# A graph layer and eight experts on one core: route and experts in one program, partial quads by their tiles

## The chip, the cores and the metric

One of the cores of a Trainium2 chip runs the whole kernel. The time is the device time of one execution in microseconds (us), taken from the core. TensorE is called PE, VectorE DVE, ScalarE ACT, GpSimd POOL and SyncE, which issues most DMAs, SP.

## The reference

The input is 12500 nodes of 256 features, with 200000 edges. A graph layer comes first, then a layer of eight experts of which each node uses one:

```python
x = x + gnn(layernorm(x), src, dst)          # gather by src, sum by dst, two products, batch norm
# then, with h = layernorm(x), C = ceil(1.25 * 12500 / 8) = 1954, D = 256, F = 1024:
probs = softmax(h @ gate_w + gate_b);  idx = argmax(probs);  prb = probs[idx]
pos = running count of idx;  kept = pos < C
buf = zeros((8, C, D)).at[idx, pos].set(h, mode='drop')
hmid = relu(einsum('ecd,edf->ecf', buf, w1) + b1[:, None, :])
ybuf = einsum('ecf,efd->ecd', hmid, w2) + b2[:, None, :]
x = x + nan_to_num(ybuf[idx, pos] * (prb * kept)[:, None])
```

By these inputs the experts get 1091, 1033, 3008, 980, 2266, 2418, 1025 and 679 nodes; at most 1954 of each are kept. In tiles of 128 nodes that is 9, 9, 16, 8, 16, 16, 9 and 6, or 89 in all.

## The kernel before

The program has four stages one after another: norm and edges (the graph layer, up to 1745 us in the profile), route (up to 1955 us) and experts (the rest).

**Route** (`stage_route`, L1142 on) goes over the nodes in quads of 4 tiles. It works out gate and position, stores the node itself to `out`, and scatters each node's row (features, statistics, node number, logits) to its slot in the DRAM buffer `slot_rows` (POOL, L1263), 512 slots to a quad and 4 quads to an expert. At its end SP issues the load of expert 0's weights (`load_expert`, L1136 to L1139) and waits for it. The stage is a block of its own: at the block's end (L1211) each engine drains its queue and all engines meet.

**Experts** (`stage_experts`) is a second block. SP loads the first slot's word of each tile (`first_row`, L1641), and DVE makes of them the number of used tiles of each expert, kept in `words`. Then 32 steps, one per quad, run on five engines with semaphores between them. The helper `walk` writes the order out: 8 steps, a loop of one round of 8 steps run twice (L130), and the last 8 steps with what drains. In a step each engine does its parts in the written order, each part for the quad that lies its lag behind:

```python
sp:   [(load, 0), (weights, 3)]                         # x_row in; next expert's weights
dve:  [(norm, 0), (meta, 0), (first_weights, 0), (split, 4), (finish, 3), (low_columns, 0)]
pe:   [(turn, 0), (product_up, 1), (product_down, 2)]
act:  [(expo, 0), (columns, 0), (hidden, 1), (split, 3)]
pool: [(low_hidden, 1), (scatter, 3)]
```

A quad goes through: `norm` (DVE L1827, `x_xn`, 4 instructions), `turn` (PE L1695, 8 transposes to PSUM `x_turned`), `columns` (ACT L1757, `x_xTh`, the f16 half), `low_columns` (DVE L1849, `x_xTl`, the rest), `product_up` (PE L1711, 8 chunks of 6 matmuls, as wide as the arm's tiles), `hidden` (ACT L1778, two activations a chunk), `low_hidden` (POOL L1659, `x_midl`), `product_down` (PE L1735, 24 matmuls a tile), `finish` (DVE L1878 to L1893: `yb` with the bias, `y` with the gate's share, then the guard for infinities and the sum into `x_res`) and `scatter` (POOL L1674, 4 indirect DMAs to `out`). The turn of quad s waits for `x_xn` of s and `x_xTl` of s-1; the down product of s waits for `yb` of s-1, since PSUM `x_down` holds one quad. `first_weights` and `split` divide an expert's weights in two f16 halves (ACT L1801, L1802; DVE L1841, L1843).

**Arms.** The number of used tiles is known to the engines only at run time. `branch` (L1597 to L1607) reads it and runs a quad or skips it. On PE alone there are two arms with code of their own, 4 tiles or 2. With the tile counts above PE works 4, 4, 2, 0 tiles in the quads of experts 0, 1 and 6, 4, 4, 0, 0 in expert 3, 4, 2, 0, 0 in expert 7, and 4 in each quad of the others: 92 tiles. The other engines work 25 full quads and skip 7; POOL scatters for all 32.

## Time and profile before

| | |
|---|---|
| median of 3 runs (lowest, highest) | 2583.26 us (2576.55, 2584.69) |
| the profiled execution, its span | 2588.4 us, 2586.6 us |
| mean granted clock of PE | 0.838 |
| PE, DVE, ACT, POOL busy | 1715.5, 1463.4, 693.4, 1737.4 us |

The profiled execution is one run more; its span is what its profile shows, and 1.8 us lie around it. A granted clock of 1 is TensorE's full 2.4 GHz, 0.5 is 1.2 GHz. Two thirds of the span are the graph layer, which the change leaves alone but for where buffers lie; what matters here is from 1740 us on. Below, a start time is in us from the start of the span, a name as `x_up<-x_xTh,x_w1h` says what is written out of what, a square bracket at the end is the engine's idle time before the row and what ended it, and engines with a q (PEq, POOLq) are their sequencers: there stand branches, drains and waits, which don't count as busy.

### The profile page before, as it was taken

The page shows a single profiled execution, that of the slowest core. Times are in us where ns is not written, and L with a number is a line of the kernel's source. Part 1 is how long each engine was busy: PE and PEld are TensorE (multiplying, and loading weights), DVE is VectorE, ACT ScalarE, POOL GpSimd, SP SyncE. Part 2 cuts the span into 40 slices and gives each one's busy share as a digit, 9 for nine tenths or more (in the row PEclk, how much of TensorE's full clock was granted, in tenths as well). Part 3 has the DMA queues.
Part 4 walks back from the last instruction along what each step waited for, and adds up shares of the span by engine and source line. Part 5 has one row for each costly group of instructions (what it writes and reads, how often), then busy time and mean ns, then how long its engine had stood idle before and what let it go on. Part 6 is the DMA issues. An engine that isn't in the chain of part 4 may idle for free. (4 is left out here: it accounts for less than half of the span.)

```text
span 2586.6 us, 32984 instructions
## 1 busy us (share of the span) xinstructions
PE 1715.5 (66%) x9167; PEld 1048.3 (41%) x9168; DVE 1463.4 (57%) x4301; ACT 693.4 (27%) x1092; POOL 1737.4 (67%) x1716
## 2 busy tenths in 40 slices
PE   0055446565667666677677777666656789899984
PEld 0033223233333333333333434345544556656663
DVE  7886632655247425633643333237873786857894
ACT  6910000100010001001110111116654545355552
POOL 1177777777777777777777776723563767677876
PEclk9986678777778888888789989986667989999997
DMA  7644466545744665466356433326753211222120
GB/s 231 237 135 119 122 202 204 158 131 171 234 153 123 192 221 151 131 199 213 96 171 211 128 105 93 105 50 209 222 164 106 88 49 56 94 84 72 49 93 13
DMA packets 202983, 361.16 MB, mean 140 GB/s; under 512 B 63573, under 2 KB 127403, under 8 KB 202790
## 3 DMA queue, kind: packets, MB, share of 16 engines
q0 software_dynamic: 70464, 185.02, 24.0%
q1 hardware_dynamic: 130182, 172.61, 20.6%
q8 instruction: 110, 1.80, 0.3%
q10 hardware_dynamic: 2144, 1.05, 0.2%
q14 instruction: 83, 0.68, 0.1%
HBM read 291.08 MB, written 75.58 MB: 142 GB/s over the span
## 5 line engine op out<-in xcount | busy, mean ns | idle before, releaser
L743 POOL DMA_INDIRECT e_got<-table,e_idx x1240 | 1188.4, 958 | 426.8 <-issue 366.2
L820 PE MATMUL e_sums<-e_got,e_hot 128*128 128x256 f16 x1920 | 358.2, 366 | 482.0 <-DMA e_got<-table,e_idx 276.7
L820 PEld LDWEIGHTS e_sums<-e_got,e_hot 128*128 128x128 f16 x1920 | 239.1, 128 | 606.0 <-DMA e_got<-table,e_idx 305.4
L1003 DVE SCALAR_TENSOR_TENSOR nodes<-e_sums,above,nodes 128x256 f32 (+1 forms) x161 | 77.3, 480 | 610.7 <-PE e_sums L820 396.1
L1659 POOL TENSOR_TENSOR x_midl<-x_midf,x_midh 128x512 f16<-128x512 f32 x200 | 294.3, 1498 | 97.6 <-ACT x_midh L1778 93.4
L926 ACT ACTIVATE e_hT<-e_up 128x1024 f32<-128x1024 f32 (+1 forms) x25 | 25.2, 1006 | 1074.8 <-PE e_up L869 1074.8
L1067 DVE TENSOR_TENSOR counts<-counts,e_tally 128x490 f32 x220 | 159.5, 725 | 127.7 <-PE e_tally L848 115.7
L1735 PE MATMUL x_down<-x_w2h,x_midh 128*128 128x256 f16 x736 | 205.4, 279 | 20.1 <-DVE x_yb L1878 8.1
L1735 PE MATMUL x_down<-x_w2h,x_midl 128*128 128x256 f16 x736 | 205.4, 279 | 0.0
L1735 PE MATMUL x_down<-x_w2l,x_midh 128*128 128x256 f16 x736 | 205.4, 279 | 0.0
L1674 POOL DMA_INDIRECT out<-x_res,x_nodei x128 | 144.9, 1132 | 88.4 <-DVE x_res L1893 49.7
L877 PE MATMUL e_up<-e_hT,W1s 128*128 128x512 f32 (+1 forms) x400 | 180.7, 606 | 28.6 <-ACT e_hT L926 28.6
L1017 DVE TENSOR_SCALAR e_hot<-ring,e_rel 128x128 f16 x960 | 175.5, 272 | 32.8 <-DVE e_rel L1011 32.5
L883 PE MATMUL e_up<-e_mid,W2s 128*128 128x512 f32 (+1 forms) x400 | 174.9, 590 | 19.2 <-ACT e_mid L929 19.2
L858 PE MATMUL e_tally<-w1f,counts 128*128 128x512 f16 x490 | 140.9, 428 | 49.4 <-DMA w1f<-table 48.3
L1263 POOL DMA_INDIRECT slot_rows<-r_row,r_slots x100 | 97.6, 976 | 92.6 <-DVE r_slots L1490 68.8
L1711 PE MATMUL x_up<-x_xTh,x_w1h 128*128 128x512 f16 (+1 forms) x400 | 149.3, 373 | 2.1 <-ACT x_midh L1778 2.1
L1711 PE MATMUL x_up<-x_xTh,x_w1l 128*128 128x512 f16 (+1 forms) x400 | 148.5, 371 | 2.3 <-issue 2.3
L1711 PE MATMUL x_up<-x_xTl,x_w1h 128*128 128x512 f16 (+1 forms) x400 | 148.8, 372 | 0.9 <-issue 0.9
L1778 ACT ACTIVATE x_midf<-x_up,x_b1s 128x512 f32<-128x512 f32 x200 | 138.7, 693 | 23.9 <-PE x_up L1711 15.5
L1778 ACT ACTIVATE x_midh<-x_up,x_b1s 128x512 f16<-128x512 f32 x200 | 137.6, 688 | 0.0
L848 PE MATMUL e_tally<-w2f 128*128 128x490 f16 x328 | 114.6, 458 | 28.4 <-DVE w2f L1056 27.3
(214 smaller groups left out, 2837.4 us busy)
## 6 DMA issues: line engine op xcount, KB each, us to landing
w1f<-table SPq DMA_DIRECT2D x120, 512.0 KB, 4.6
e_got<-table,e_idx POOLq DMA_INDIRECT x1240
slot_rows<-e_zero SPq DMA_DIRECT2D x64, 268.0 KB, 3.2
x_row<-slot_rows SPq DMA_DIRECT2D x32, 536.0 KB, 7.3
table<-n_pair SPq DMA_DIRECT2D x25, 512.0 KB, 2.9
counts<-in_x SPq DMA_DIRECT2D x24, 512.0 KB, 4.5
r_xin<-in_x SPq DMA_DIRECT2D x24, 512.0 KB, 5.0
out<-r_row SPq DMA_DIRECT2D x24, 512.0 KB, 3.2
```

The lines of the kernel that those rows point to most:

```text
L743: pool.indirect_dma_start(got[:, r, t, :], None, table.rearrange("p h d -> (p h) d"), bass.IndirectOffsetOnAxis(ap=idx[:, r, t:t + 1], axi ...
L820: ins = nc.tensor.matmul(sums[:, place, 0:D], hot[:, place, t, :], got[:, r, t, half * D:(half + 1) * D], start=(t == 0 and half == 0), st ...
L858: ins = nc.tensor.matmul(product, counts[:, k0 + k, 0:P], part[:, number % 2, k, :], start=(k0 + k == 0), stop=(k0 + k == HI - 1))
L877: ins = nc.tensor.matmul(up[:, c % 2, 0:width], W1s[:, j, c * P:(c + 1) * P], hT[:, j, 0:width], start=(j == 0), stop=(j == DK - 1))
L883: ins = nc.tensor.matmul(up[:, c, 0:width], W2s[:, j, c * P:(c + 1) * P], mid[:, j, 0:width], start=(j == 0), stop=(j == H1C - 1))
L1017: ins = nc.vector.tensor_scalar(hot[:, place, t, :], plan.ring[:, ring_at(shift)], rel[:, place, t:t + 1], None, ALU.is_equal)
L1067: nc.vector.tensor_tensor(place, place, tally[:, group % BANKS, 0:KEY].rearrange("p (k d) -> p k d", d=TW), ALU.add).then_inc(s_count, 1)
L1659: nc.gpsimd.tensor_tensor(midl[:, j % 2, c, :], midf[:, c % MB, :], midh[:, j % 2, c, :], ALU.subtract).then_inc(s_mlo, 1)
L1674: pool.indirect_dma_start(out, bass.IndirectOffsetOnAxis(ap=nodei[:, j, t:t + 1], axis=0), res[:, r, t, :], None, bounds_check=bound, oob_ ...
L1711: ins = nc.tensor.matmul(up[:, c % MB, 0:tiles * P], w[:, h, k, cols], x[:, j % 2, k, 0:tiles * P], start=(n == 0), stop=(n == len(passes) ...
L1735: ins = nc.tensor.matmul(down[:, t, :], m[:, j % 2, k, rows], w[:, h, k, :], start=(n == 0), stop=(n == len(passes) - 1))
L1778: ins = nc.scalar.activation(m, up[:, c % MB, :], ACT.Relu, bias=b1s[:, h, c:c + 1], scale=MID_SCALE / (X_SCALE * W_SCALE))
```

## The change

1. **One program.** Route's per-engine code becomes functions (`route.sync(sp)`, `route.tensor(pe)` and so on), which each engine runs ahead of its expert code in one block; the meeting of engines at L1211 is gone. Instead SP waits for the landing of `out` and of the scatters, and then issues `b2s` and the first `x_row`. The weights of expert 0 are issued at the start of route, and split there (ACT, DVE) into the memory `halves`, which the two stages and the graph layer share. The tile counts are worked out in route from its own counters.
2. **Norm and columns a step ahead.** All that follows `norm` lags a step more.
3. **The gate's share in the product out of PSUM.** `yb` and `y` become one step `product`, 4 instructions (a tile each) with the factor `share`; bias times share comes from ACT (`x_b2p`, 4 activations after `hidden`). The down product of s waits for it.
4. **Partial quads by their tiles.** `branch` takes a number of steps: 4 arms on PE, 2 for `hidden`, `low_hidden` and `finish`, 1 for `product` and `scatter`. A scatter of an unused quad sends 16 rows in place of 128.

```diff
-        with nc.Block() as block:
-            @block.sync
-            def _(sp):
-                sp.dma_start(gw[:, :, :], gate_w.rearrange("(k p) e -> p k e", p=P)).then_inc(s_gw, 16)
+        def route_sync(sp):
+            sp.dma_start(gw[:, :, :], gate_w.rearrange("(k p) e -> p k e", p=P)).then_inc(s_gw, 16)
+            load_expert(sp, nc, w1, xb1, w2, w1f, w2f, b1f, 0, s_w)
...
-                load_expert(sp, nc, w1, xb1, w2, w1f, w2f, b1f, 0, s_w)
-                sp.wait_ge(s_w, 48)
+            for j in range(R5):
+                sp.wait_ge(s_scat[j], 16 * QT * (NQ // R5))
...
-            def branch(own, j, work, skip, narrow=False):
+            def branch(own, j, work, skip, steps=1):
                 if j == 0:
                     engine.reg_mov(own, word)
                 used = engine.snap(engine.snap(own) % 32) if j < SG else engine.snap(engine.snap(own) // 32)
-                with engine.If(used > j % SG * QT):
-                    if narrow:
-                        with engine.If(used > j % SG * QT + QT // 2):
-                            work(QT)
-                        with engine.Else():
-                            work(QT // 2)
-                    else:
-                        work()
-                with engine.Else():
-                    skip()
+                base = j % SG * QT
+                def between(low, high):
+                    if high - low == 1:
+                        return work(high * QT // steps) if high else skip()
+                    middle = (low + high + 1) // 2
+                    with engine.If(used > base + (middle - 1) * QT // steps):
+                        between(middle, high)
+                    with engine.Else():
+                        between(low, middle)
+                between(-1, steps)
...
-                    branch(ups, j, work, skip, narrow=True)
+                    branch(ups, j, work, skip, QT)
...
-                            pe.wait_ge(s_yv, s * 7 - 6)
+                            pe.wait_ge(s_yv, (s - 1) * GUARD + 1)
...
-                walk(pe, [(take, 0), (turn, 0), (product_up, 1), (product_down, 2)], NS, R8)
+                walk(pe, [(take, 0), (turn, 1), (product_up, 2), (product_down, 3)], NS, R8)
...
+                        for t in range(QT):
+                            ins = nc.scalar.activation(b2p[:, j % 2, t, :], b2s[:, h, :], ACT.Identity,
+                                                       scale=prob[:, j, t:t + 1])
+                        ins.then_inc(s_b2p, 1)
...
-                walk(act, [(take, 0), (expo, 0), (columns, 0), (hidden, 1), (split, 3)], NS, R8)
+                walk(act, [(take, 0), (expo, 0), (columns, 1), (hidden, 2), (split, 4)], NS, R8)
...
+                def product(s, j, rnd):
+
+                    def work(tiles):
+                        dve.wait_ge(s_down, s + 1)
+                        dve.wait_ge(s_b2p, s + 1)
+                        if not (isinstance(s, int) and s == 0):
+                            dve.wait_ge(s_res, s)
+                        for t in range(tiles):
+                            ins = nc.vector.scalar_tensor_tensor(out=y[:, t, :], in0=down[:, t, :], scalar=share[:, j, t:t + 1],
+                                                                 in1=b2p[:, j % 2, t, :], op0=ALU.mult, op1=ALU.add)
+                        ins.then_inc(s_yv, 1)
...
-                walk(dve, [(take, 0), (norm, 0), (meta, 0), (first_weights, 0), (split, 4), (finish, 3), (low_columns, 0)], NS, R8)
+                walk(dve, [(take, 0), (product, 4), (low_columns, 1), (norm, 0), (meta, 0), (split, 5), (finish, 4)], NS, R8)
```

SP's order around the two boundaries. Before, expert 0's weights stand at the end of route, ahead of the block's end and the first loads of the experts:

```order
L1136 DMA w1f<-in_w 128x2x1024
L1137 DMA w2f<-in_w 128x8x256
L1139 DMA b1f<-in_xb 128x8x1
L1211 UNCONDITIONAL_BRANCH
L1613 UNCONDITIONAL_BRANCH
L1641 DMA x_first_row<-slot_rows 1x128x1
L1632 DMA x_b2s<-in_xb 128x256
L1637 DMA x_row<-slot_rows 128x4x268 x4
```

After the change SP begins route so:

```order
L1262 DMA r_gw<-in_gate_w 128x2x8
L1263 DMA r_gb<-in_gate_b 128x8
L1183 DMA w1f<-in_w 128x2x1024
L1184 DMA w2f<-in_w 128x8x256
L1186 DMA b1f<-in_xb 128x8x1
L1273 DMA r_xin<-in_x 128x4x256 x4
L1283 DMA out<-r_row 128x4x256
```

The weights have moved from behind route's last store to ahead of its first input, `r_xin`.

PE's up product of the first quad. Before, the arm of 4 tiles (512 wide) ends in a jump over the arm of 2 tiles:

```order
L1711 MATMUL x_up<-x_xTh,x_w1h 128x512
L1711 MATMUL x_up<-x_xTl,x_w1h 128x512
L1711 MATMUL x_up<-x_xTh,x_w1l 128x512
L1601 UNCONDITIONAL_BRANCH
L1711 MATMUL x_up<-x_xTh,x_w1h 128x256
L1711 MATMUL x_up<-x_xTl,x_w1h 128x256
L1711 MATMUL x_up<-x_xTh,x_w1l 128x256
```

After, PE's full arm of the same quad ends so (in `halves` lie the weights, and the rows with ISA are waits):

```order
L1790 MATMUL x_up<-x_xTl,halves 128x512
L1790 MATMUL x_up<-x_xTh,halves 128x512
L1667 UNCONDITIONAL_BRANCH
L1782 ISA
L1787 ISA
L1790 MATMUL x_up<-x_xTh,halves 128x384
```

Further on, still on PE, the arm of 3 tiles ends and that of 2 tiles begins, with a compare between them:

```order
L1790 MATMUL x_up<-x_xTl,halves 128x384
L1790 MATMUL x_up<-x_xTh,halves 128x384
L1669 UNCONDITIONAL_BRANCH
L1667 COMPARE_AND_BRANCH
L1782 ISA
L1787 ISA
L1790 MATMUL x_up<-x_xTh,halves 128x256
```

Last comes PE's arm of 1 tile, and behind it the skip (L1797) and the compares of the down product:

```order
L1790 MATMUL x_up<-x_xTl,halves 128x128
L1790 MATMUL x_up<-x_xTh,halves 128x128
L1667 UNCONDITIONAL_BRANCH
L1797 ISA
L1669 UNCONDITIONAL_BRANCH
L1660 ISA
L1667 COMPARE_AND_BRANCH x2
```

What has moved is where a jump leads: from the full arm PE now goes past three arms of 48 matmuls (144), before past one; in the down product past arms of 72, 48 and 24 matmuls (144 too), before past one of 48. A quad that is skipped goes past all four arms.

DVE's step in the first round. Before, the step of quad 3 and on reads so from its norm to the norm of the next:

```order
L1827 TENSOR_SCALAR x_xn<-x_row 128x256 x4
L1858 TENSOR_REDUCE x_tot<-x_ex 128x4
L1859 TENSOR_SCALAR x_gone<-x_row 128x4
L1862 RECIPROCAL x_prob<-x_tot 128x4
L1863 SCALAR_TENSOR_TENSOR x_nodei<-x_row,x_gone 128x4
L1597 ISA
L1599 COMPARE_AND_BRANCH
L1878 SCALAR_TENSOR_TENSOR x_yb<-x_down,x_b2s 128x1024
L1881 TENSOR_TENSOR x_y<-x_yb,x_prob 128x1024
```

After, DVE's step (at quad 4's norm) begins with the product of an earlier quad, and the guard of `finish` comes last:

```order
L1963 SCALAR_TENSOR_TENSOR x_y<-x_down,x_share,x_b2p 128x256 x4
L1667 UNCONDITIONAL_BRANCH
L1932 SCALAR_TENSOR_TENSOR x_xTl<-x_turned,x_xTh 128x1024
L1910 TENSOR_SCALAR x_xn<-x_row 128x256 x4
L1941 TENSOR_REDUCE x_tot<-x_ex 128x4
L1942 TENSOR_SCALAR x_gone<-x_row 128x4
L1945 RECIPROCAL x_prob<-x_tot 128x4
L1946 SCALAR_TENSOR_TENSOR x_nodei<-x_row,x_gone 128x4
L1949 TENSOR_SCALAR x_share<-x_prob 128x4
L1659 ISA
L1667 COMPARE_AND_BRANCH
L1986 TENSOR_SCALAR x_up<-x_y 128x1024
```

The read of PSUM `x_down` has moved to the step's head, ahead of `x_xTl` and `x_xn`; in the first quad of an expert it has no compare ahead of it, since its threshold is below any count.

## Rows read from the trace of the kernel before

**Rows 1.** Stretches: us, busy (and count) by engine, PE clock, DMA share, GB/s.
```profile
1745.00:1955.00 210.00, 115.41 (x1125) 100.23 (x1125) 156.34 (x680) 119.20 (x201) 100.40 (x105) 0.60 0.59 187
1955.00:2587.00 632.00, 538.18 (x3664) 373.66 (x3664) 450.19 (x512) 313.45 (x480) 440.67 (x329) 0.92 0.22 71
```

**Rows 2.** One line of ACT, 2410 to 2480 us: four full steps.
```profile
L1757 ACT ACTIVATE x_xTh<-x_turned x4: 1024/1024/1024, 2413.5 to 2478.7; 128x1024 f16<-128x1024 f32 x4
```

**Rows 3.** What PE waited for, 2000 to 2560 us: total, times, longest.
```profile
PE x_turned L1695 <- DVE x_xn L1827: 25.8, 6, 5.9
PE x_down L1735 <- DVE x_yb L1878: 8.1, 2, 4.1
PE x_down L1735 <- DVE x_dn L1885: 7.4, 2, 4.4
PE x_down L1735 <- PEq L1719: 4.6, 1, 4.6
```

**Rows 4.** The block's end, line L1211: count, ns min/median/max, start.
```profile
L1211 POOLq COMPARE_BRANCH  x1: 43/43/43, 1941.3 to 1941.3; - x1
L1211 POOLq DRAIN  x1: 8223/8223/8223, 1941.5 to 1941.5; - x1
```

**Rows 5.** Timeline from route's last scatter to the first quad.
```profile
1939.16 0.97 POOL L1263 DMA_INDIRECT slot_rows<-r_row,r_slots  x1 [0.30 <-issue]
...
1950.65 0.58 SPq L1632 DMA_DIRECT2D x_b2s<-in_xb  x1
...
1960.73 1.02 ACT L1757 ACTIVATE x_xTh<-x_turned 128x1024 f16<-128x1024 f32 x1 [2.63 <-PE x_turned L1695]
...
1961.29 2.28 DVE L1843 SCALAR_TENSOR_TENSOR x_w2l<-w2f,x_w2h 128x2048 f16<-128x2048 f32 x1
...
1963.50 1.22 DVE L1849 SCALAR_TENSOR_TENSOR x_xTl<-x_turned,x_xTh 128x1024 f16<-128x1024 f32 x1
```

**Rows 6.** Timeline of SP's DMAs at the start of route.
```profile
1741.46 2.21 SPq L1224 DMA_DIRECT2D r_xin<-in_x  x4
1753.25 0.38 SPq L1234 DMA_DIRECT2D out<-r_row  x1
```

**Rows 7.** What SP waited for, 1745 to 2587 us, one row.
```profile
SPq L1211 <- DMA b1f<-in_xb: 8.4, 1, 8.4
```

**Rows 8.** End of the work, timeline of POOL: first and last of 12 scatters.
```profile
2566.60 0.97 POOL L1674 DMA_INDIRECT out<-x_res,x_nodei  x1 [5.23 <-DVEq L1903]
...
2580.66 0.97 POOL L1674 DMA_INDIRECT out<-x_res,x_nodei  x1 [0.30 <-issue]
```

**Rows 9.** Groups by shape, 1955 to 2587 us: busy, mean ns, idle before.
```profile
L1735 PE MATMUL x_down<-x_w2h,x_midl 128*128 128x256 f16 x736 | 205.4, 279 | 0.0
...
L1881 DVE TENSOR_TENSOR x_y<-x_yb,x_prob 128x1024 f32<-128x1024 f32 x25 | 30.7, 1228 | 0.9
L1878 DVE SCALAR_TENSOR_TENSOR x_yb<-x_down,x_b2s 128x1024 f32<-128x1024 f32 x25 | 30.6, 1223 | 81.0 <-PE x_down L1735 80.6 <-issue 0.2
```

**Rows 10.** Timeline of PE, two up matmuls of a full arm.
```profile
1989.08 0.38 PE L1711 MATMUL x_up<-x_xTh,x_w1l 128*128 128x512 f16 x1
1989.30 0.38 PE L1711 MATMUL x_up<-x_xTh,x_w1h 128*128 128x512 f16 x1
```

**Rows 11.** PE's branches, by line and stretch: count, ns min/median/max, start.
```profile
L1601 PEldq COMPARE_BRANCH  x92: 65/171/3139, 1966.4 to 2547.6; - x92
...
L1601 PEldq COMPARE_BRANCH  x1: 3048/3048/3048, 2019.7 to 2019.7; - x1
...
L1599 PEldq COMPARE_BRANCH  x1: 5692/5692/5692, 2236.6 to 2236.6; - x1
...
L130 PEldq COMPARE_BRANCH  x1: 4992/4992/4992, 2254.5 to 2254.5; - x1
```

**Rows 12.** Timeline of PE, the first turn behind the loop's edge.
```profile
2260.54 0.88 PE L1695 MATMUL x_turned<-ident,x_xn 128*128 128x128 f32 x3 [4.40 <-issue]
```

**Rows 13.** DMA queues, 1955 to 2587 us: packets, MB, share; one row.
```profile
q8 instruction: 68, 1.11, 0.8%
```

More of the change, by code:

```diff
@@ new lines, in route_gpsimd, with scatter @@
+        def route_gpsimd(pool):
+            nc.gpsimd.memset(row[:, :, :, D + 3:D + 4], 0.0).then_inc(s_rows, 1)
+            nc.gpsimd.memset(seen[:, :, :], 0.0).then_inc(s_const, 1)
+            nc.gpsimd.iota(rev[:, :], pattern=[[-1, NX]], base=NX, channel_multiplier=0,
+                           allow_small_or_imprecise_dtypes=True).then_inc(s_const, 1)
+            nc.gpsimd.iota(node1[:, :], pattern=[[P, NB]], base=1, channel_multiplier=1,
+                           allow_small_or_imprecise_dtypes=True).then_inc(s_const, 1)
+            nc.gpsimd.memset(ones[:, :], 1.0).then_inc(s_ones, 1)
+            pool.wait_ge(s_ones, 1)
+            nc.gpsimd.affine_select(out=tri[:, :], in_=ones[:, :], compare_op=ALU.is_ge, fill=0.0,
+                                    base=0, pattern=[[1, P]], channel_multiplier=-1).then_inc(s_tri, 1)
+            bound = pool.to_reg(NX * SLOTS - 1)
+            def scatter(q, j):
+                pool.wait_ge(s_slot, q + 1)
+                for t in range(QT):
+                    pool.indirect_dma_start(
+                        buf, bass.IndirectOffsetOnAxis(ap=slots[:, j, t:t + 1], axis=0), row[:, j, t, :], None,
+                        bounds_check=bound, oob_is_err=False).then_inc(s_scat[j], 16)
+            pool.wait_ge(s_rows, 1)
+            for q in range(NQ):
+                scatter(q, q % R5)
@@ L1504, in last_slots @@
+                if before:
                     placed(p, 2)
@@ L1638, in load @@
                                  buf[at(s, QN), :].rearrange("(t p) d -> p t d", p=P)).then_inc(s_row[j], 16)
-                with nc.allow_non_contiguous_dma(reason="one word of the first slot of each tile"):
-                    sp.dma_start(first_row[:, :, :], buf.rearrange("(e g n) d -> n e g d", g=SG * QT, n=P)[0:1, :, :, D + 2]
-                                 ).then_inc(s_first, 16)
                 bias(0, 0)
-                walk(sp, [(load, 0), (weights, 3)], NS, R8)
+                walk(sp, [(load, 0), (weights, 4)], NS, R8)
             @block.gpsimd
             def _(pool):
-                ready = counter(pool, "x_ready", R8 + 1 - 3)
+                route.gpsimd(pool)
+                ready = counter(pool, "x_ready", R8 + 1 - 4)
                 take, branch = tile_counts(pool)
                 lows = pool.alloc_register("lows_word")
+                sent = pool.alloc_register("sent_word")
                 bound = pool.to_reg(N - 1)
                 def low_hidden(s, j, rnd):
-                    def work():
+                    def work(tiles):
+                        cols = slice(0, tiles * P)
                         if not (isinstance(s, int) and s < 2):
@@ L1742, in skip @@
                         pe.sem_inc(s_down, 1)
-                    branch(downs, j, work, skip, narrow=True)
-                walk(pe, [(take, 0), (turn, 0), (product_up, 1), (product_down, 2)], NS, R8)
+                    branch(downs, j, work, skip, QT)
+                walk(pe, [(take, 0), (turn, 1), (product_up, 2), (product_down, 3)], NS, R8)
             @block.scalar
             def _(act):
+                route.scalar(act)
                 take, branch = tile_counts(act)
```

703 lines of the change are left out of this document (372 added, 331 removed).

## The prediction, made before the changed kernel ran

> **What bounds the kernel now.** I first read the stretches [rows 1]: the change touches route (210 us) and experts (632 us), and in the experts PE is busy for 538 of 632 us at a granted clock of 0.92, against 450 for DVE and 441 for POOL. Then the full steps: ACT's `x_xTh` comes every (2478.7 - 2413.5) / 3 = 21.7 us [rows 2]. Two up matmuls start 0.22 apart [rows 10], so 48 of them take 10.4; with 0.9 for the turn that leaves 10.4 for 96 down matmuls, 0.11 each. That is the whole step: a full quad is PE's own work, and nothing off PE shortens it. What can be won lies where PE waits. Its list of waits has 25.8 us for `x_xn`, 8.1 for `yb`, 7.4 that are put down to `x_dn` (also the finish chain of DVE) and 4.6 for its own skip [rows 3], together 46, all at experts with a short last quad. The rest is at the ends: the gap between route and experts [rows 4, 5], and the row of scatters at the end [rows 8].
>
> **Route's end: -9.4.** POOL's last scatter is issued at 1939.16 [rows 5], and POOL sees all of them landed at 1941.3; then its drain takes 8.22 us [rows 4], the engines meet, and SP issues `b2s` at 1950.65 [rows 5], ahead of the first `x_row`. After the change SP waits for the landings itself and issues `b2s` at once: 1950.65 - 1941.3 = 9.35. POOL now makes its memset after that, beside the load and the norm of the first quad, so it costs nothing; were it on the path, it could not cost more than the drain gave. Bounds: -9.4 if the memory order on SP adds nothing, -7 if its landing is seen later.
>
> **Weights ahead of route's input: +1.5.** The order shows 2 MB of weights ahead of `r_xin`. Before, `r_xin` went out at 1741.46 and the first store at 1753.25 [rows 6]; the load of the weights at route's end kept SP waiting 8.4 us [rows 7] with nothing else running, hidden then behind POOL's scatters. Its three issues cost SP about 1.4, and its transfer shares the queues with the first inputs. Low bound 0, high bound 6 (most of the 8.4, if the first input gets what the weights leave). I take 1.5, since in route the first input has 12 us to its first store and only the start of the pipeline can be late.
>
> **First quad: -1.7.** `x_xTh` ends at 1961.75, but `x_xTl` starts at 1963.50, behind the split of `w2l` [rows 5]. The split is now done in route, so 1.75 goes.
>
> **Tail: -4.** From the first of 12 scatters to the last is 14.1 us, 1.28 each [rows 8]. After, the last 12 are 8 full ones and 4 of 16 rows. If these cost half, that is -2.6; and on the way to the last `x_res` DVE has `yb` and `y` (1.22 and 1.23 [rows 9]), in whose place come four quarter-width ones, at best 1.3: -1.2. Bounds -1 and -6.
>
> **Tiles: what the arms do.** I work the threshold out with `used` as tiles left at a quad's start, u. For 4 steps the arm of 4 runs if u > 2, that of 3 if u > 1, of 2 if u > 0 and of 1 if u > -1. So u = 1 gets two tiles as before, u = 2 gets three, u = 0, an empty quad, gets one, and no quad works fewer tiles than before. The 736 rows a pass [rows 9] are 92 tiles of 8; after it is 94, or 752. For two steps u = 1 is a full quad, u = 0 half of one; with one step all quads but two run `product` and scatter. So what the words say of partial quads doesn't happen. It costs: expert 7's second quad has a third tile, 24 down matmuls and 48 wider ups, 2.6 + 2.6 = 5.2. Expert 3's third quad, skipped before, becomes a quad of one tile: turn to finish through all engines, about 5 for 48 narrow ups and 2.6 for the down, +7.6, less the skip it had (4.6 [rows 3]), plus its entries (next part).
>
> **Jumps on PE.** Most compares cost 0.065 to 0.17 us, but the line's longest are 3.14, and single ones 3.05 and 5.69; the loop's edge takes 4.99 [rows 11]. The 3.05 and the 3.14 lead into the arm of 2 tiles of a down product, past 96 matmuls; the 5.69 is a skip. Jumps past the 48 matmuls of the up arm stay at the short end. How much of it PE feels: the edge's branch is reached at 2254.5, PE runs dry at 2260.54 - 4.40 = 2256.14 [rows 11, 12], so the sequencer is 1.6 us ahead after a down product, about 15 matmuls, which is 3.3 us after an up product. In the same stretch 68 packets, 1.11 MB, of instructions came in [rows 13], 16 KB each: code is fetched as it is reached. After the change every full arm ends in a jump past 144 matmuls, in both products; skips go past 192 and 240. The up's is covered (3.0 against 3.3). The down's could show 3.0 - 1.6 = 1.4 in 21 full quads, 29 us; the low end is 0, since the rows have a 4-tile exit only past 48. I take 5, near the low end, because the long costs above come where one jump follows closely on another, which a full step's don't. Short tails are where jumps follow each other: before, two long ones a tail; after, about two more in each of experts 0, 1 and 6 (into the 2-tile up arm, past its skip), 3 x 2 x 3.0 = +18, and two more each in experts 3 and 7, +6 each.
>
> The Trainium skill ("Runtime: NRT & Kernel Launch", "Instruction fetch mechanics") says that a taken branch whose target isn't in the current window of two pages of 256 instructions waits for a fetch. By that rule the jumps past 144 matmuls stall and my +35 stands; the same section gives PE 2048 instructions of memory, by which a jump of some 300 would be free and the sum 35 lower.
>
> **What DVE gives back: -20.** The norm a step ahead and the early read of PSUM aim at the 41 us of `x_xn`, `yb` and `x_dn` [rows 3]. Low bound -41. But the turn of s still waits for `x_xTl` of s-1, and in a short tail the finish chain stays on DVE in the same step, so part only changes its name; and a stall that a jump causes hides a wait for DVE. High bound 0; I take half, 20.
>
> ACT's four `x_b2p` activations, a quarter as wide as its `x_xTh`, which takes 1.02 [rows 2], are at most 4 us a quad; ACT is idle half of the 632 us [rows 1], so 0, and if that cover failed, 4 us in a tail.
>
> **Sum.** Ends: -9.4 + 1.5 - 1.7 - 4 = -13.6. Experts: expert 3 +7.6 - 4.6 + 6 = +9; expert 7 +5.2 + 6 = +11; full steps +5; other tails +18; DVE -20: together +23. In all +9.4, call it +10. Against the profiled 2588.4 that is 2598; the median of the runs shown is 5.1 lower, so 2593 us there.
>
> **The rivals.**
> - *Jumps are free, and it is faster.* The median of 0.17 us over 92 branches speaks for it, the 3.05 and 3.14 against. Then +5, +18 and 12 of the entries go: 2593 - 35 = 2558; with DVE giving only 10 back it is 2568, with the full 41 it is 2537. I put it at about 2563. It decides if a jump past 144 matmuls costs under 1 us more than before. Chance 0.23.
> - *Gains and losses meet.* Norm a step ahead covers the fetches: DVE gives 30 back in place of 20, or two of the three equal tails hide their jumps (-12): 2581 to 2583. Chance 0.2.
> - *Fetches meet the weights' loads.* The 5.69 against 3.05 shows what a fetch costs beside other DMAs; the load of an expert falls in the short tails' steps. With 2.6 more for 8 of them, or 1.4 for the 21 exits: 2593 + 21 to 24 = 2615. Chance 0.17.
> - *The thresholds are right after all*, 89 tiles: five tiles less at some 5.2 each (2.6 down, 2.6 up), the one-tile quad's among them, -26: 2567. The code's line speaks against it. Chance 0.02.
>
> The forecast has 0.38. A measurement here can't tell 0.3%, 8 us, from no change: 2575.5 to 2591 is "same". Faster takes the first rival, the last and a little of the second, 0.26; same the second's rest and the forecast's low side, 0.25; slower 0.49. The range reaches from 2560, within the first rival, to 2616.
>
> **What would show it.** Right: no drain between scatter and `b2s`, about 10 us less there; x752 in the rows of `x_down`; PE's branches on `between`'s lines with some 25 or more of 2 to 3 us; PE waiting less for `x_xn` but having new gaps put down to its sequencer or to issue; experts' full steps still 21.7 to 22; the last four scatters shorter. More instruction packets (over 68). Wrong: branches all short, or full steps of 23; a late first store in route (over 1760 on the old scale); a first PE wait list with `x_b2p` behind it.

## The result, and the profile after

The changed kernel takes 2653.99 us (median; 2648.19 to 2659.60), against 2583.98 before: a ratio of 1.0269, 95% interval 1.0251 to 1.0286. It is slower by 70 us. The forecast was 2593, slower, with a range up to 2616: the sign was right and the size far off.

The profiled execution took 2659.6 us. Its stretches from route's first DMA on, in the columns of [rows 1]:

```profile
1745.00:1955.00 210.00, 117.14 (x1137) 100.92 (x1135) 163.82 (x692) 124.05 (x207) 102.04 (x106) 0.64 0.59 187
1955.00:2657.00 702.00, 556.83 (x3784) 383.42 (x3784) 483.12 (x617) 357.18 (x598) 407.91 (x339) 0.90 0.21 66
```

The experts take 70 us more, and PE is busy for only 19 of them (557 against 538): PE waits more. The starts of single instructions give the division. All times are differences between rows of the two timelines:

| stretch | before | after | difference |
|---|---|---|---|
| graph layer, to route's first DMA | 1740.5 | 1749.1 | +8.6 |
| route and boundary, to the first turn | 218.2 | 218.6 | +0.4 |
| first turn to the end of the last down product ("the experts' stretch") | 599.3 | 660.0 | +60.7 |
| from there to the end | 28.6 | 29.9 | +1.3 |

Both kernels were profiled once more later, on other chips. The changed kernel's experts' stretch is 660.5 us there, the kernel before's 591.6. So the 599.3 of the table is uncertain by some 8 us, and the loss in this stretch is 61 to 69 us. Versions of the changed kernel with the same expert code agree better: 581.4, 581.6 and 581.9 in three runs below.

What PE waited for in the changed kernel, from the first turn to the last down product (the first row's 24.8 is the wait ahead of the very first turn):

```profile
PE x_turned L1774 <- DVE x_xn L1910: 28.5, 2, 24.8
PE x_down L1814 <- issue: 26.3, 7, 8.7
PE x_turned L1774 <- issue: 23.9, 9, 8.2
PE x_turned L1774 <- PEq L1821: 19.2, 4, 7.2
PE x_down L1814 <- DVE x_fine L1988: 11.4, 1, 11.4
PE x_down L1814 <- POOL x_midl L1724: 6.4, 5, 3.3
PE x_up L1790 <- issue: 6.1, 8, 2.1
PE x_down L1814 <- PEq L1798: 5.4, 1, 5.4
```

Put beside [rows 3]: the waits for `x_xn` are down from 25.8 to 3.7 within the stretch, as meant. In their place stand "issue" and PEq, PE's own sequencer, with 81 us in all. Waits put down to DVE's finish chain and to POOL are 18, about as much as before's 15.5. The branches of PE, in the columns of [rows 11] (L1667 is the compare in `between`, L131 the loop's edge), and the instruction queue of the stretch from 1967 to 2628 us:

```profile
L1667 PEldq COMPARE_BRANCH  x190: 65/178/6470, 1973.5 to 2641.0; - x190
L131 PEldq COMPARE_BRANCH  x5: 67/214/8699, 1815.2 to 2440.8; - x5
q8 instruction: 113, 1.85, 1.3%
```

Counted in the trace, 45 branches of PE in the experts took over 1 us, 156 us together; before it were 14 with 43 us. That these waits are for code can be seen in the same trace: of the 41 long branches up to the last down product, 37 have the start of a 16 KB packet of the instruction queue inside, of the 149 shorter ones 5. Two of the gaps that they make on PE, the first behind the loop's edge:

```profile
2268.21 1.11 PE L1774 MATMUL x_turned<-ident,x_xn 128*128 128x128 f32 x4 [8.17 <-issue]
...
2115.58 0.39 PE L1814 MATMUL x_down<-halves,x_midh 128*128 128x256 f16 x1 [8.56 <-issue]
```

The number of tiles, by shape over 1955 to 2657 us (columns of [rows 9]; 32 instructions of `x_xTh` make a quad):

```profile
L1814 PE MATMUL x_down<-halves,x_midl 128*128 128x256 f16 x760 | 211.6, 278 | 0.0
...
L1790 PE MATMUL x_up<-x_xTh,halves 128*128 128x512 f16 x672 | 205.4, 382 | 0.4 <-issue 0.4
...
L1790 PE MATMUL x_up<-x_xTh,halves 128*128 128x384 f16 x64 | 19.2, 384 | 1.7 <-issue 1.7
L1790 PE MATMUL x_up<-x_xTh,halves 128*128 128x256 f16 x64 | 13.4, 306 | 2.1 <-issue 1.5 <-ACT x_midh L1859 0.6
...
L1790 PE MATMUL x_up<-x_xTh,halves 128*128 128x128 f16 x32 | 5.0, 304 | 2.1 <-issue 2.1
```

That is 21 quads of 4 tiles, two of 3, two of 2 and one of 1: 95 tiles. The thresholds do what the prediction read in them; the 95th tile is expert 6's, which ran three where I had counted two. With right thresholds (below) it runs two, and PE 90 tiles in all: the program counts 10 used tiles in expert 6, where the inputs give 9. Where the tenth comes from is open.

At the boundary, two things collide that the forecast had at nothing or as a gain. A scatter of route beside DVE's split of expert 0's weights, which now runs there, and further on the first `x_xn` beside POOL's memset:

```profile
1943.45 2.27 DVE L1576 SCALAR_TENSOR_TENSOR halves<-w1f,halves 128x2048 f16<-128x2048 f32 x1
...
1944.02 4.76 POOL L1310 DMA_INDIRECT slot_rows<-r_row,r_slots  x1 [0.30 <-issue]
...
1954.20 0.97 POOL L1310 DMA_INDIRECT slot_rows<-r_row,r_slots  x1 [0.31 <-issue]
1956.35 0.35 SPq L1697 DMA_DIRECT2D x_b2s<-in_xb  x1
...
1962.73 4.89 DVE L1910 TENSOR_SCALAR x_xn<-x_row 128x256 f32<-128x256 f32 x4 [14.80 <-DMA x_row<-slot_rows]
...
1963.00 3.50 POOL L1755 MEMSET x_res<- 128x4096 f32 x1
...
1967.67 1.97 PE L1774 MATMUL x_turned<-ident,x_xn 128*128 128x128 f32 x8 [24.79 <-DVE x_xn L1910]
```

The scatter takes 4.76 in place of 0.97, and the four `x_xn` 4.89, where four undisturbed ones take 1.37.

### The profile page after: what moved, and what is told of

It reads as the page before. It is cut to its first block and busy times, and to the rows that moved or that the text cites. A ratio compares the mean times of both kernels' runs of the same rounds, so it can differ in the third digit from the quotient of the medians.

```text
span 2657.6 us, 33753 instructions
## 1 busy us (share of the span) xinstructions
PE 1751.4 (66%) x9288; PEld 1061.2 (40%) x9289; DVE 1501.7 (57%) x4409; ACT 739.7 (28%) x1212; POOL 1706.0 (64%) x1725
## 5 line engine op out<-in xcount | busy, mean ns | idle before, releaser
L773 POOL DMA_INDIRECT halves<-table,halves x1240 | 1188.2, 958 | 431.2 <-issue 364.5
L850 PE MATMUL e_sums<-halves 128*128 128x256 f16 x1920 | 361.6, 367 | 474.7 <-DMA halves<-table,halves 269.3
L850 PEld LDWEIGHTS e_sums<-halves 128*128 128x128 f16 x1920 | 239.8, 129 | 603.4 <-DMA halves<-table,halves 301.4
L1724 POOL TENSOR_TENSOR x_midl<-x_midf,x_midh 128x512 f16<-128x512 f32 (+1 forms) x208 | 279.7, 1369 | 96.1 <-ACT x_midh L1859 90.8
L1814 PE MATMUL x_down<-halves,x_midh 128*128 128x256 f16 x1520 | 260.3, 279 | 49.6 <-issue 26.3
L1790 PE MATMUL x_up<-x_xTh,halves 128*128 128x512 f16 (+3 forms) x832 | 243.0, 373 | 6.2 <-issue 5.6
L1814 PE MATMUL x_down<-halves,x_midl 128*128 128x256 f16 x760 | 211.6, 278 | 0.0
L1047 DVE TENSOR_SCALAR halves<-ring,e_rel 128x128 f16 x960 | 175.3, 273 | 33.0 <-DVE e_rel L1041 32.7
L1814 PEld LDWEIGHTS x_down<-halves,x_midh 128*128 128x128 f16 x1520 | 150.5, 100 | 75.0 <-issue 38.4
L1790 PE MATMUL x_up<-x_xTl,halves 128*128 128x512 f16 (+3 forms) x416 | 155.2, 373 | 0.6 <-issue 0.5
L867 PE MATMUL e_sums<-halves 128*128 128x256 f16 x640 | 93.4, 308 | 61.1 <-DMA halves<-table,halves 34.0
```

Of the source, the lines that this page charges most:

```text
L773: pool.indirect_dma_start(got[:, r, t, :], None, table.rearrange("p h d -> (p h) d"), bass.IndirectOffsetOnAxis(ap=idx[:, r, t:t + 1], axi ...
L850: ins = nc.tensor.matmul(sums[:, place, 0:D], hot[:, place, t, :], got[:, r, t, half * D:(half + 1) * D], start=(t == 0 and half == 0), st ...
L1047: ins = nc.vector.tensor_scalar(hot[:, place, t, :], plan.ring[:, ring_at(shift)], rel[:, place, t:t + 1], None, ALU.is_equal)
L1724: nc.gpsimd.tensor_tensor(midl[:, j % 2, c, cols], midf[:, c % MB, cols], midh[:, j % 2, c, cols], ALU.subtract).then_inc(s_mlo, 1)
L1790: ins = nc.tensor.matmul(up[:, c % MB, 0:tiles * P], w[:, h, k, cols], x[:, j % 2, k, 0:tiles * P], start=(n == 0), stop=(n == len(passes) ...
L1814: ins = nc.tensor.matmul(down[:, t, :], m[:, j % 2, k, rows], w[:, h, k, :], start=(n == 0), stop=(n == len(passes) - 1))
```

## The experiments

Theory J: PE waits for its own code after jumps, and the four arms make the jumps longer, more frequent and closer together. Rival W: the loss is by the added work (tiles, an extra quad), the product's form, the lags or the one program. The experiments ran on four chips. On two of them the graph layer took some 550 us longer for every kernel, before's too, so totals are given as ratios to the kernel before on the same chip, and stretches from the profiles. The same microseconds make a smaller ratio on those two, where before takes 3166 to 3172 us: the changed kernel's 70 us would be 1.022 there.

**The kernel before once more** (`before_again`). Expected: 599 us in the experts' stretch again, within 2. Measured: 591.6, on the chip of `old_order` and `ends_fixed`. The expectation failed, and what is measured against before's stretch below is uncertain by these 8 us. The rest agrees better: route and boundary 220.2 us (218.2), the tail 28.6 in both.

**Dead arms in the kernel before** (`dead_arms`). In PE's branch of the kernel before:

```diff
                         with engine.Else():
-                            work(QT // 2)
+                            with engine.If(used > 100):
+                                work(3)
+                            with engine.Else():
+                                with engine.If(used < 200):
+                                    work(QT // 2)
+                                with engine.Else():
+                                    work(1)
```

> The kernel before, with two more arms (3 tiles and 1 tile) in each of PE's branches, placed as in the changed kernel and never entered; the work is that of before, only the jumps are longer (past 144 matmuls at a full arm's end in place of 48) and the code per step grows from about 300 to 500 matmuls. Theory J (PE waits for code after jumps): 30 to 50 us slower than before, all of it between the first and the last quad of the experts, most at experts with a short tail and at the loop's edge. Rival W (the changed kernel lost its time by more work, other waits and the new order): within 8 us of before.

Measured: 1.0057 (1.0022 to 1.0091), which is 18 us (7 to 29). The experts' stretch is 625.2 us against 599.3 (591.6 in before's second profile), and PE has 26 branches over 1 us, 102 us together. Same work to the instruction, and yet these waits and this code traffic in the stretch:

```profile
PE x_turned L1701 <- issue: 16.0, 5, 4.5
PE x_down L1741 <- DVE x_fine L1892: 12.9, 2, 6.6
PE x_turned L1701 <- PEq L1748: 9.8, 2, 8.0
...
q8 instruction: 88, 1.44, 1.1%
```

The kernel before has 66 instruction packets in its stretch, this one 88, the changed one 113. Code that never runs costs 26 to 34 us by the stretches; the total gives less, and its interval begins just under W's bound of 8 and ends just under J's 30. The branches and packets speak for J, but this alone isn't the loss.

**Two arms in the changed kernel** (`two_arms`).

```diff
-                between(-1, steps)
+                with engine.If(used > base):
+                    if steps == QT:
+                        with engine.If(used > base + QT // 2):
+                            work(QT)
+                        with engine.Else():
+                            work(QT // 2)
+                    else:
+                        work(QT)
+                with engine.Else():
+                    skip()
```

> The changed kernel with the old choice of arms: 4 or 2 tiles on PE, whole quads on the other engines, and every engine skips an empty quad. Theory J: most of the 60 us that the experts' stretch lost comes back, the time is 2585 to 2605. Rival W, in so far as the loss is by the new order, the share in the product or the one program: it stays above 2630.

Measured: 0.994 (0.9896 to 0.9983), a little faster than before. The experts' stretch is 581.9: 78 less than the changed kernel and 10 to 17 less than before. 14 long branches, 41 us. So all of the loss in this stretch is in the choice of arms, and the rest of the change is a gain there. (The expected totals were for a chip on which before takes 2584; what answers to them is the difference to before in us, here 19 less, 5 to 33: below the expected range.)

**Right thresholds** (`right_bounds`).

```diff
-                    with engine.If(used > base + (middle - 1) * QT // steps):
+                    with engine.If(used > base + middle * QT // steps):
```

> The changed kernel with thresholds moved up by one step, so that a quad with u tiles left runs exactly u of them (PE), or the half or whole that covers them; code and jumps stay as long. Against the changed kernel it has 5 or 6 tiles less on PE, no quad for an empty one, and fewer whole quads on ACT, POOL and DVE. Theory J: only the work goes, 10 to 25 us faster than the changed kernel, 2630 to 2644. Rival W: the added work and what it drags with it was the loss, 2600 or less.

Measured: 1.014 (1.0073 to 1.0207), on this chip 44 us (23 to 66) more than before; the stretch is 657.0, only 3 less than the changed kernel's, with 47 long branches, 172 us. The 3 us are what is left of two larger changes. PE is busy for 538.4 us in the stretch in place of 556.8: five tiles less take 18 us off its busy time. But it stands idle for 118.6 in place of 103.2. The added tiles did cost; taking them away brought other arms and more waiting in their place.

**Route in a block of its own** (`own_block`), shown for SP and the same on each engine:

```diff
         with nc.Block() as block:
             @block.sync
             def _(sp):
                 route.sync(sp)
...
+        with nc.Block() as block:
+            @block.sync
+            def _(sp):
                 def weights(s, j, rnd):
```

> The changed kernel with route in a block of its own again, so that all engines drain and meet between route and experts; everything else as changed. If one program saved the 9.4 us of drain and meeting, this is 8 to 10 us slower than the changed kernel (2662 to 2664). If another wait at the same place (SP's for the scatters) took its place, it is 0 to 4 us slower.

Measured: 1.022 (1.0156 to 1.0284). The changed kernel itself did not run on this chip, so the total can't answer; the stretches can. From the start of the last scatter to `b2s` it takes 9.5 us in this kernel and 2.2 in `right_bounds`, on the same chip; to the first turn route takes 239.2 against 232.9. So the one program does save the drain, 7.3 us of which 6.3 arrive. The experts' stretch is 668.0, 8 more than the changed kernel's with the same expert code; why is open.

**One compare first** (`skip_first`): right thresholds, and an empty quad goes straight to its skip.

```diff
-                between(-1, steps)
+                with engine.If(used > base):
+                    between(0, steps)
+                with engine.Else():
+                    skip()
```

> The changed kernel with the thresholds right, and with one compare first that sends an empty quad straight to its skip, in place of a chain through the arms; the four arms stay. Of PE's branches over 1 us there were 45 in the changed kernel, 47 with right thresholds alone, 26 with two dead arms in the old chain, 14 before. If the chain of far jumps at skips makes the difference between 26 and 47, about 30 are left and the experts' stretch is 620 to 630 us (657 without this edit). If the length of the arms alone counts, 40 or more and 645 or more.

Measured: 1.0198 (1.0166 to 1.023); stretch 644.9, 40 long branches, 165 us. 12 us come back; I had expected 27 to 37. The chain of compares is the smaller part. (The branches' sum doesn't follow the stretch closely: it is 165 us here and 156 in the changed kernel, whose stretch is 15 us longer but holds 17 us more of PE's busy time.)

**The old lags** (`old_order`), with two arms:

```diff
-                walk(pe, [(take, 0), (turn, 1), (product_up, 2), (product_down, 3)], NS, R8)
+                walk(pe, [(take, 0), (turn, 0), (product_up, 1), (product_down, 2)], NS, R8)
...
-                walk(dve, [(take, 0), (product, 4), (low_columns, 1), (norm, 0), (meta, 0), (split, 5), (finish, 4)], NS, R8)
+                walk(dve, [(take, 0), (norm, 0), (meta, 0), (split, 4), (product, 3), (finish, 3), (low_columns, 0)], NS, R8)
```

> Two arms on PE and whole quads, as in the run with two arms, but every part at its old lag (turn with norm, product and finish at 3); one program and the share in the product stay. With two arms and the new lags the experts' stretch was 582 us against 599 before. If norm and columns a step ahead bring it, this goes back to 595 to 600; if the product out of PSUM does, it stays at 582 to 586.

Measured: 1.002 (1.0002 to 1.0037); stretch 597.1. Its waits are those of before:

```profile
PE x_turned L1774 <- DVE x_xn L1910: 27.6, 8, 5.3
PE x_down L1814 <- DVE x_y L1963: 16.8, 3, 5.9
```

So norm and columns a step ahead bring 15 us. Between 597.1 and before's 599.3 or 591.6 no effect of the product's new form can be told.

**Dead arms in the new order** (`dead_new`): the edit of `dead_arms` on top of `two_arms`.

> Two arms and the new lags (experts' stretch 582 us), with two more arms in each of PE's branches that are never entered; ACT, POOL and DVE stay at whole quads. Theory J in its strong form (PE's code alone makes the loss of the changed kernel): the stretch becomes 620 to 645, about 2620 in all. If the dead arms cost only what they did in the kernel before (26 to 33 us), it becomes 608 to 615, and the rest of the loss is by the chain of compares and by the arms that run.

Measured: 1.0014 (0.9973 to 1.0054); the stretch is 610.1, 28 more than with two arms, 27 long branches with 102 us. (The profiled execution lies 1.4% over its kernel's median. The excess is in the graph layer, which ends at 2344.8 us, against 2286.8 and 2303.4 in the other two kernels on this chip; and `no_last_still` on it, with two arms, has 581.6 in the stretch.) The weak form holds: dead arms make 28 of the 78.

**Halves on the other engines** (`halves_only`): two arms on PE, and for ACT, POOL and `finish` a second arm for two tiles, by the compare that PE has:

```diff
+                    elif steps == 2:
+                        with engine.If(used > base + QT // 2):
+                            work(QT)
+                        with engine.Else():
+                            work(QT // 2)
```

> Two arms on PE, and half or whole quads (with right thresholds) on ACT, POOL and in finish; it is the other half of the edit on arms. Theory J: 575 to 585 us in the experts' stretch against 582, since these engines' branches never took over 1 us in any run. If the second arm on these engines costs like PE's, 595 or more.

Measured: 0.9955 (0.9924 to 0.9986); stretch 577.4, 4.5 less than without. These engines' branches never took 1 us in any run.

**Four live arms on PE alone** (`pe_four`), the other engines at whole quads:

```diff
+                        with engine.If(used > base + 2):
+                            with engine.If(used > base + 3):
+                                work(4)
+                            with engine.Else():
+                                work(3)
+                        with engine.Else():
+                            with engine.If(used > base + 1):
+                                work(2)
+                            with engine.Else():
+                                work(1)
```

> Two arms, new lags and whole quads on the other engines as in the run with two arms, but four arms on PE that do run (1 to 4 tiles, right thresholds, one compare first for the empty quad). Two dead arms gave an experts' stretch of 610, four live ones with halves on the other engines 645. If entering the narrow arms deeper in the code makes the 35 us between them, this is 640 to 650; if the halves and single-step branches of the other engines did, about 610.

Measured: 1.0191 (1.0155 to 1.0227); stretch 647.4, 40 long branches with 164 us. The branches of the quads, and PE's waits:

```profile
L1663 PEldq COMPARE_BRANCH  x64: 65/75/5320, 1959.2 to 2607.6; - x64
...
L1666 PEldq COMPARE_BRANCH  x84: 65/173/8620, 1959.4 to 2581.8; - x84
```

```profile
PE x_down L1820 <- issue: 32.5, 11, 8.5
...
PE x_turned L1780 <- issue: 27.1, 8, 8.4
PE x_turned L1780 <- PEq L1827: 21.9, 5, 7.4
```

The 35 us between dead and live arms are PE's alone: the run works 90 tiles in place of 92, and takes 37 us longer than with two dead arms. Against them it differs in which arm a short quad enters and by a compare more in each used quad; no run parts these two.

**The boundary** (`ends_fixed`), with two arms:

```diff
             dve.wait_ge(s_tiles, 2)
...
+            for j in range(R5):
+                dve.wait_ge(s_scat[j], 16 * QT * (NQ // R5))
             dve.wait_ge(s_whi, 1)
...
-            load_expert(sp, nc, w1, xb1, w2, w1f, w2f, b1f, 0, s_w)
...
+            walk(sp, [(load, 0), (store, 3), (first_weights, 4)], NQ, R5)
...
-                nc.gpsimd.memset(res[:, :, :, :], 0.0).then_inc(s_still, 1)
```

> Two arms and whole quads with the new lags, and three edits at the boundary: expert 0's weights go out behind route's fourth input, DVE splits them after route's scatters have landed, and POOL no longer clears x_res (nothing reads it unwritten when whole quads are skipped). From route's first DMA to the first turn: the split beside a scatter cost 3.8 us (a scatter of 4.76 in place of 0.97), the memset beside x_xn 2.6 to 3.2, the weights ahead of the input 1 to 2.7. So 7 to 9 us less than with two arms alone; if these were not on the path, under 2. The total should lie 20 to 30 us below before, the fastest so far.

Measured: 0.9943 (0.9921 to 0.9965), 2567.91 us. Against `old_order` on the same chip, whose boundary is the changed kernel's, the way to the first turn is 208.7 us in place of 216.4: 7.7 less. The rows:

```profile
1936.51 0.97 POOL L1313 DMA_INDIRECT slot_rows<-r_row,r_slots  x1 [0.30 <-issue]
1938.66 0.35 SPq L1702 DMA_DIRECT2D x_b2s<-in_xb  x1
1938.89 2.28 DVE L1581 SCALAR_TENSOR_TENSOR halves<-w1f,halves 128x2048 f16<-128x2048 f32 x1
...
1944.53 1.44 DVE L1914 TENSOR_SCALAR x_xn<-x_row 128x256 f32<-128x256 f32 x4 [1.16 <-DMA x_row<-slot_rows]
```

The split now lies under the load of `x_row`, no scatter is long, and `x_xn` takes 1.44. 4.2 of the 7.7 come ahead of the end of the last scatter (200.1 against 204.3), 3.6 behind `b2s`. In the first, 3.8 are the long scatter; for the place of the weights 0.4 are left.

**No scatters for the last expert's empty quads** (`no_last_still`), on top of it:

```diff
-                    branch(sent, j, work, skip)
+                    branch(sent, j, work, (lambda: None) if isinstance(s, int) and s >= NS - SG else skip)
...
-                for j in range(RW):
+                for j in range(RW - SG):
                     pool.wait_ge(s_scat[j], 16 * QT * (NS // RW))
+                for j in range(RW - SG, RW):
+                    branch(sent, j, lambda tiles: pool.wait_ge(s_scat[j], 16 * QT * (NS // RW)),
+                           lambda: pool.wait_ge(s_scat[j], 16 * QT * (NS // RW - 1)))
```

> The run with the ends mended, and the empty quads of the last expert issue no scatter at all (the last wait is chosen by the same count). Its tail had eight small scatters at 1.15 us and then a drain of 10.5 us where before had 3.3. Without the eight, 9.2 us of issue go; the drain goes back to 3.3 if it is the small ones that make it. So 9 to 17 us less than the 2568 of the run with the ends mended: 2551 to 2559.

Measured: 0.989 (0.9845 to 0.9936), on this chip 35 us (20 to 49) less than before; 25 to 33 were expected. From the last down product to the end it takes 26.3 us, 8.5 less than `ends_fixed`. POOL's last drain stayed at 10.5, without a small scatter near it, so that it is the small ones that make it long is refuted.

**All together** (`best_halves`): this, and the edit of `halves_only` with halves in the scatters too:

```diff
-                    branch(sent, j, work, (lambda: None) if isinstance(s, int) and s >= NS - SG else skip)
+                    branch(sent, j, work, (lambda: None) if isinstance(s, int) and s >= NS - SG else skip, 2)
```

> The fastest run's edits (two arms on PE, new lags, ends mended, no scatters for the last expert's empty quads) and halves on ACT, POOL, in finish and in the scatters. Halves alone took 4.5 us from the experts' stretch. Expected 3 to 6 us less than without them, 0.5% to 2% faster than before; if POOL's small scatters for the upper halves cost what the halves give, no less.

Measured: 0.9854 (0.9826 to 0.9883), 2549.93 us: the fastest version, 1.5% faster than before. The interval touches that of `no_last_still`, so that it beats it is not shown by the totals. Its experts' stretch is 572.7, its tail 23.8. That is 11.4 us less in these two stretches than without halves (581.6 and 26.3, on another chip), more than the 3 to 6 expected.

**The changed kernel once more** (`after_again`).

> The changed kernel, unchanged, once more: its graph layer was 8.6 us longer than before's in the profiled executions, though only its buffers moved. If that was one execution's chance, the layer now ends within 4 us of where the other kernels of its family have it, and the experts' stretch is 655 to 662 again.

Measured: 1.025 (1.0215 to 1.0286); the stretch is 660.5. The graph layer ends at 1744.7 (1749.1 in the first profile). Of the kernels with the same graph layer on chips of this speed the others end it at 1735.3 to 1740.3, before's two at 1736.6 and 1740.5. So about half of the 8.6 was chance; 4 us more than any other, in two executions, are not settled.

## Why the prediction was wrong, point by point

**The step that failed is the price of the jumps on PE.** The prediction put +5 on the full steps, +18 on the three equal tails and 12 on the entries of experts 3 and 7: 35 us. With its tiles (5.2 and 7.6, less 4.6 for a skip) that makes 43 between two arms and the changed kernel. Measured, it is 78 us. From `two_arms` to the changed kernel PE's idle time in the stretch rises by 53 us (50 to 103) and its busy time by 25 (531.9 to 556.8). By the prediction's own prices for tiles, 18 of the 25 are work, expert 6's third tile included; so the jumps cost about 60 us (an estimate, 78 less 18) in place of 35. What is not idle time in them fits a slower PE: 92 tiles take 531.9 us at a granted clock of 0.95 in `two_arms`, and 90 tiles take 538.4 at 0.90 in `right_bounds`.

Divided by the steps of the edit, the 78 are 28 for arms that only lie in the way (`dead_new`), 35 for arms of PE that do run (`pe_four`, `skip_first`), 12 for the chain of compares ahead of a skip (`skip_first` against `right_bounds`), and 3 for the wrong thresholds, work and saved waits taken together.

The mechanism was the one named; two sizes in it were too small, and a third, the loop's edge, had no term:

- *Full steps.* From the turn of quad 19 to that of quad 27 before takes 173.7 us, the changed kernel 180.0 (2350.80 to 2530.78): 0.8 a step against the 0.25 taken; the bound given was 1.4. The price is not one of every jump: of the 16 exits past 144 matmuls in these eight steps 5 took 3.3 to 3.8 us, the other 11 0.3 to 0.4, like the exits past 48 before. What decides which ones wait is open.
- *The loop's edge.* It takes 8.7 us in place of 4.99, and PE stands for 8.2 in place of 4.4. The prediction's sum has no term for it. In the second profile it takes 7.3.
- *Tails.* Two more long jumps a tail were counted, on top of two before. Before's trace has only one over 1 us in each of the tails of experts 0 and 1 (at 2019.7 and 2094.4), and in the changed kernel there are 31 more in all. Against two arms the tails of experts 0, 1 and 3 (with the edge) and the end cost 11, 15, 20 and 20 us more. A gap of 8.56 us like the one shown is three of them in a row (3.5, 3.0 and 2.8 us, from 2105.0 on), with nothing queued on PE between.

Part of the miss lies outside the experts' stretch. The profiled executions differ by 71 us, and the sum had 9. Of the 62 us between these, 39 are in the experts' stretch, 9 in the graph layer, for which the prediction had no term, 8 ahead of the first turn and 5 in the tail.

The Trainium skill ("Runtime: NRT & Kernel Launch", "Instruction fetch mechanics") says that a taken branch out of the current two pages of instructions waits for a fetch, and the traces agree: 66, 88 and 113 packets of code, and 43, 102 and 156 us of long branches, for the same or nearly the same work, and most of the long branches with the start of a packet inside (11 of 13, 21 of 24 and 37 of 41 up to the last down product). Its figure of 2048 instructions of memory for PE, by which the rival "jumps are free" would have come true, doesn't show in any run here.

**What DVE gives back:** -20 forecast, 15 measured (`old_order` against `two_arms`, and 15.7 against `ends_fixed` on the same chip). This is the lags alone; the early read of PSUM by the new product adds nothing that can be told. The half was a choice between the bounds 0 and 41, so that it came near is partly luck.

**Tiles:** right in what the arms do (94 tiles forecast, 95 run), and one tile short in the count, expert 6's third, which makes 18 us of work of the 13. What it cost beyond its work lies in the jumps: the right thresholds, which take all this work away, gave 3 us back (`right_bounds`).

**The drain:** -9.4 forecast. From the start of the last scatter to `b2s` it was 11.5 us and is 2.15, -9.3. Right.

**First quad:** -1.7 forecast. From the first turn to the first up matmul 9.1 us before, 7.4 after. Right. But the split that left this place now stands beside a scatter, and costs 3.8 there.

**Memset of `x_res`, costed at nothing:** wrong, +3.2. The prediction named as its cover the load and the norm of the first quad; it comes when the load has landed, and the norm doesn't cover it but is held up by it. In the kernel before it ran at 1952.95, under the load; the changed kernel lets it wait for the first `x_row`. From `b2s` to the first turn 8.1 us before, 11.3 after, 7.4 in `ends_fixed`.

**Weights ahead of route's input:** +1.5 forecast; 0.4 by `ends_fixed`, within what executions differ (the last scatter is 199.6 and 201.5 us behind route's start in two executions of before).

**Tail:** -4 forecast, +1.3 measured. The small scatters are 1.15 us apart in place of 1.28: with 16 rows they cost nearly what 128 do, not half. And the last quads' scatters begin later:

```profile
2638.26 0.97 POOL L1738 DMA_INDIRECT out<-x_res,x_nodei  x1 [11.57 <-DVEq L2005]
```

The last `x_res` ended at 2635.2, 3 us before; in the kernel before the first of these followed it within 0.3. In the 3 us DVE, which still runs `product` for an empty quad, waits for PE's skip; that this is what holds the scatter is not shown:

```profile
2637.30 1.66 DVE L1963 SCALAR_TENSOR_TENSOR x_y<-x_down,x_share,x_b2p 128x256 f32<-128x256 f32 x4 [2.11 <-PEq L1821]
```

The rivals fell as forecasts: jumps are not free, the gains and losses did not meet, and the thresholds are not right. "Fetches meet the weights' loads" came nearest, at 2615. No run here moved the loads, but the changed kernel's trace bears its mechanism out in part. The three longest branches (8.7, 6.5 and 5.7 us, at 2258, 2333 and 2078) stand behind loads that SP issues at 2256, 2330 and 2071, and the DMA engines are busy for 0.90 to 0.96 of them; at the loop's edge before, which took 4.99, it was 0.14. Of the 41 long branches, the 12 beside at least 15% of traffic other than code take 4.1 us in the mean, the other 29 3.2; that is about 11 us in all, half of what the rival had put on it.

## What to carry to other kernels

On an engine that works from long unrolled code, an arm costs its place even if it never runs: count the jumps, and how many follow one another with nothing queued, before adding arms to save tiles. Choose the arms for each engine by its code: halves gave 4.5 us on ACT, POOL and DVE, four arms on PE cost 65 us, for two tiles less. A kernel profiled twice can differ by 8 us in a stretch: profile the kernel before twice too, before small gains are read from it. Work that is moved under a gap isn't free if it holds up what ends the gap: look at what runs beside it, as the split beside POOL's scatter and the memset beside DVE's norm here, and put it where the other engine waits.

## What the runs showed of the hardware that was not expected

- Of PE's 45 long branches in the changed kernel 34 took 2.5 to 3.9 us, the longest 8.7 at the loop's edge (9.1 in `own_block`); none on ACT, POOL, DVE took over 1 us in the same kernels.
- A POOL indirect DMA beside a DVE instruction on two SBUF operands (2.27 us each, two in a row) took 3.8 us more; one DVE instruction beside a POOL memset of 3.5 us took 3.93 in place of 0.4. With both moved away in `ends_fixed` neither was long.
- Two exits of the same length can differ tenfold: past 144 matmuls, 0.3 to 0.4 us or 3.3 to 3.8.
- An indirect DMA with 16 rows takes POOL 0.84 to 0.86 us, with 128 rows 0.97.
- POOL's drain at the program's end is 3.33 us in four kernels (before, changed, dead arms in before, own block) and 10.52 in all the others, the same to some ns each time; what decides is open.
